# Attention loops with bodies of 12 quads in place of 4, and one rule for the score banks

## The chip, the cores and the metric

The kernel runs on one core of a Trainium2 chip. The metric is the device time of one execution in microseconds (us). The profile names the engines PE (TensorE matmuls), PEld (TensorE weight loads, which overlap PE, and with them TensorE's instruction sequencer), DVE (VectorE), ACT (ScalarE), POOL (GpSimd) and SP (SyncE).

## The reference, cut to what matters

A layer of differential attention is followed by an expert layer. Nearly all the time goes to the attention over 16 batches of 1024 tokens, with 32 score heads each (two for each of the 16 value heads):

```python
scores = jnp.einsum('bhqd,bhkd->bhqk', q, k)          # 16 x 32 heads, 1024 x 1024, hd = 8
probs = jax.nn.softmax(scores.astype(jnp.float32), axis=-1).astype(scores.dtype)
probs = probs.reshape(b, H, 2, s, s)
w = probs[:, :, 0] - lam * probs[:, :, 1]
attn = jnp.einsum('bhqk,bhkd->bhqd', w, v)
```

Behind it come an RMS norm per head, the output projection, two layer norms and the experts.

## The kernel before, in words

The stages run one after another: project (q, k and v), attend, route, experts, scatter. Only attend is touched. It works in quads of four score heads; 16 x 32 / 4 = 128 quads follow one another. Of a quad, each engine does this:

- PE, in 16 periods g = 0 to 15 of four steps x each: a score matmul of 512 columns (L894) into one of three PSUM banks `ps_e`, and a "try" matmul (L925) of the next quad into `ps_m`, whose row maxima the softmax needs. Scores and tries use different rows of the array. Twice a period four weighted sums (L911) add exponentials times v into the bank `ps_o`, two periods late (`LAG`).
- ACT takes the exponential of each score bank (L781), 64 in a quad, and copies `ps_o` out twice (L788).
- DVE takes 32 maxima (L813) of 1024 columns each, and does four short transposes (L820 twice, L825, L830).
- POOL splits the maxima into three bf16 parts and finishes the output. SP starts all DMAs: stacks of q and k four quads ahead, rows of maxima, v, totals, outputs.

The engines meet at semaphores alone. A score may be written once the exponential of the score that used the bank last is done (`exp_done`, L893); a try once the maximum of the try two before it is done (L924). Inside a loop the value waited for depends on the loop's counter, so most waits have a register instruction of their own.

Each engine has a loop of its own, with no barrier: `loops` = 128 / 4 - 1 = 31 laps with a body of `BUFS` = 4 quads, and behind it 4 quads written out. The loops are staggered. PE's body begins at g = `HEAD` = 14 of one quad and ends at g = 13 of the quad four later.
A quad has 64 scores (`HALVES`), and 4 x 64 = 256 is one more than a multiple of three (`SLOTS`). For the bank of a score to depend only on its place in the body, `bank` gives the last two scores of the body banks 0 and 2, and `scores_since` says that they and the first two of the next lap follow the last use of their bank by 2, 4, 2 and 4 scores in place of 3.

Of the kernel before, what the change touches and what calls it, by code (L numbers as in the profile page):

```python
# [25 lines left out]
ACT = mybir.ActivationFunctionType  # L26
# [8 lines left out]
TILES = S // P  # L35
# [5 lines left out]
QUAD = 4  # L41
# [28 lines left out]
STACK_DMAS = 2 * (3 + 6)  # L70
# [10 lines left out]
class Build:  # L81
# [440 lines left out]
    def attend(self, block, semaphores):  # L522
# [7 lines left out]
        nc, io, B = self.nc, self.io, self.B  # L530
        quads = B * QKH // QUAD
# [10 lines left out]
        SIDE = TRIES // 2  # L542
        BLK = 32
        BLOCKS = HALF // BLK
        loops = quads // BUFS - 1
        PE_HEAD, ACT_HEAD, DVE_HEAD = 200, 144, 192
        with ExitStack() as ctx:
            def sb(name, shape, dt=F32):
# [41 lines left out]
            passed = sem("passed")  # L590
            crossed_done, totals_moved, sums_turned = sem("crossed_done"), sem("totals_moved"), sem("sums_turned")

            def bank(u, j):

                at = HALVES * u + j
                return {BUFS * HALVES - 2: 0, BUFS * HALVES - 1: 2}.get(at, at % SLOTS)

            def scores_since(u, j):

                return {0: 2, 1: 4, BUFS * HALVES - 2: 2, BUFS * HALVES - 1: 4}.get(HALVES * u + j, SLOTS)  # L600

            @block.sync
            def _(sp):
# [39 lines left out]
                def first_half(n, u, more):  # L643
                    if more:
                        load_rows(n + AHEAD, (u + AHEAD) % BUFS, 0)
                        load_v(n + AHEAD, (u + AHEAD) % BUFS)
                    move_totals(n, 0)
# [14 lines left out]
                for u in range(FIRST_STACKS, BUFS):  # L662
                    load_stacks(u, u)
                first_half(0, 0, True)
                with hinted(nc, sp, 0, loops) as i:
                    for u in range(BUFS):
                        n = BUFS * i + u
                        second_half(n, u, True, True)
                        first_half(n + 1, (u + 1) % BUFS, True)
                        store(n, u)  # L670
                for u in range(BUFS):
                    n = BUFS * loops + u
                    if u == BUFS - 1:
                        for half in range(2):
                            sp.wait_ge(out_stored[half], 16 * QUAD * (1 + QKH // QUAD))
                        self.first_tokens(sp)
                    second_half(n, u, u < BUFS - AHEAD, False)
                    if u + 1 < BUFS:
                        first_half(n + 1, u + 1, u + 1 < BUFS - AHEAD)
                    store(n, u)  # L680
                for u in range(2):
                    sp.wait_ge(out_stored[u], 16 * QUAD * (1 + quads // 2))

# [1 line left out]
            def _(pool):  # L685
# [72 lines left out]
                pool.wait_ge(lam_done, 1)  # L758
                start, steps = 2 * AHEAD * SPLIT_STEPS, 2 * SPLIT_STEPS + FINISH_STEPS
                with hinted(nc, pool, 0, loops) as i:  # L760
                    for u in range(BUFS):
                        turn(BUFS * i + u, True, start + steps * (BUFS * i + u))
                for u in range(BUFS):
                    n = BUFS * loops + u
                    if u == BUFS - 1:
                        self.route_constants(pool)
                    turn(n, u < BUFS - AHEAD, start + steps * n - 2 * SPLIT_STEPS * max(0, u - (BUFS - AHEAD)))

            @block.scalar
            def _(act):  # L770
                act.wait_ge(lam_dots, 1)
                nc.scalar.activation(lam_exp[:], lam_dot[:], ACT.Exp).then_inc(lam_exps, 1)
                act.sem_inc(exp_done, SLOTS)
                act.sem_inc(sums_read, 1)

                def exponentials(n, u, first, end):
                    for j in range(first, end):
                        act.wait_ge(scores_done, HALVES * n + j + 1)
                        if j % QUAD == 0:
                            act.wait_ge(sums_done, GROUPS * n + j // QUAD + 1 - E_GROUPS + E_GROUPS)  # L780
                        nc.scalar.activation(e[:, j % E_BUFS], ps_e[:, bank(u, j)], ACT.Exp,  # L781
                                             scale=SCALE).then_inc(exp_done, 1)

                def copy_sums(n, c):

                    act.wait_ge(sums_done, GROUPS * n + TILES * (c + 1) + E_GROUPS)
                    act.wait_ge(crossed_done, 2 * n + 2)
                    nc.scalar.copy(sums[:, c], ps_o[:]).then_inc(sums_read, 1)  # L788

                def turn(n, u, last):  # L790
                    exponentials(n, u, COPY_AT, HALVES // 2 + COPY_AT)
                    copy_sums(n, 0)
                    exponentials(n, u, HALVES // 2 + COPY_AT, HALVES)
                    if not last:
                        exponentials(n + 1, (u + 1) % BUFS, 0, COPY_AT)
                    copy_sums(n, 1)

                exponentials(0, 0, 0, COPY_AT)
                with hinted(nc, act, 0, loops, slot=ACT_HEAD) as i:
                    for u in range(BUFS):  # L800
                        turn(BUFS * i + u, u, False)
                for u in range(BUFS):
                    turn(BUFS * loops + u, u, u == BUFS - 1)

            @block.vector
            def _(dve):
# [60 lines left out]
                        period(n + 1, u + 1, g, next_tries, rows)  # L867

                with hinted(nc, dve, 0, loops, slot=DVE_HEAD) as i:
                    for u in range(BUFS):  # L870
                        turn(BUFS * i + u, u, True, True, True)
                for u in range(BUFS - 1):
                    turn(BUFS * loops + u, u, u < BUFS - AHEAD, u + 1 < BUFS - AHEAD, u < BUFS - AHEAD)
                self.output_weights(dve)
                turn_sums(quads - 1)

# [6 lines left out]
            def _(pe):  # L883
# [2 lines left out]
                for u in range(FIRST_STACKS):  # L886
                    pe.sem_inc(stacks_loaded[u], 16 * STACK_DMAS)

                def score(n, u, j):

                    c, kt, pair, half = j // 32, j // QUAD % TILES, j // 2 % 2, j % 2
                    rows = slice(SCORE_ROW, SCORE_ROW + PRODUCTS + PARTS)
                    pe.wait_ge(exp_done, HALVES * n + j + 1 - scores_since(u, j) + SLOTS)  # L893
                    nc.tensor.matmul(ps_e[:, bank(u, j)],  # L894
                                     k_stack[rows, u, pair, c, kt * P:(kt + 1) * P],
                                     q_stack[rows, u, pair, c, half * HALF:(half + 1) * HALF],
                                     start=True, stop=True, tile_position=(SCORE_ROW, 0)).then_inc(scores_done, 1)

                def weighted_sums(i, u, g, columns):

                    n = BUFS * i + u
                    c, kt = g // TILES, g % TILES
                    if g == 0:
                        pe.wait_ge(v_loaded[u], 16 * (i + 1))
                    if kt == 0:
                        pe.wait_ge(sums_read, 2 * n + c + 1)
                    if columns.start == 0:
# [21 lines left out]
                    if half == 1:  # L929
                        last.then_inc(tries_done, 1)  # L930

                def period(i, u, g, tries, last_quad=True, this_quad=True):

                    n = BUFS * i + u
                    i2, u2 = i + (u + AHEAD) // BUFS, (u + AHEAD) % BUFS
                    if g % TILES == 0 and this_quad:
                        pe.wait_ge(rows_loaded[g // TILES][u], 16 * (i + 1))
                    if g == 0 and tries:
                        pe.wait_ge(stacks_loaded[u2], 16 * STACK_DMAS * (i2 + 1))
                    for x in range(QUAD):  # L940
                        done = (g - LAG) % GROUPS

                        columns = {(0, False): slice(0, HALF // 2), (2, False): slice(HALF // 2, HALF),
                                   (2, True): slice(0, HALF)}.get((x, done % TILES == 0))
                        if columns is not None:
                            if g >= LAG and this_quad:
                                weighted_sums(i, u, done, columns)
                            elif g < LAG and last_quad:
                                weighted_sums(i - (u == 0), (u - 1) % BUFS, done, columns)
                        if this_quad:  # L950
                            score(n, u, QUAD * g + x)
                        if tries:
                            attempt(n + AHEAD, u2, 2 * g + x // 2, x % 2)

# [5 lines left out]
                for g in range(HEAD):  # L960
                    period(0, 0, g, True, last_quad=False)

                def turn(i, u, tries, next_tries, next_quad):
                    for g in range(HEAD, GROUPS):
                        period(i, u, g, tries)
                    for g in range(HEAD if next_quad else LAG):
                        period(i + (u + 1) // BUFS, (u + 1) % BUFS, g, next_tries, this_quad=next_quad)

                with hinted(nc, pe, 0, loops, slot=PE_HEAD) as i:
                    for u in range(BUFS):  # L970
                        turn(i, u, True, True, True)
                for u in range(BUFS):
                    turn(loops, u, u < BUFS - AHEAD, u + 1 < BUFS - AHEAD, u + 1 < BUFS)

    def route(self, block, semaphores):
# [760 lines left out]
```

## Time and profile before

| what | value |
|---|---|
| median of 3 runs | 5913.19 us (5902.31 to 5917.62) |
| span of the profiled execution, first to last instruction | 5905.1 us |
| median less that span | 8.1 us |
| PE busy | 5596.0 us (95%) |
| DVE busy | 5463.9 us (93%) |
| ACT busy | 4958.8 us (84%) |
| POOL busy | 2055.8 us (35%) |
| instruction fetches of queue q8 | 457 packets, 7.49 MB |

Shares are of the span. Matmuls overlap one another, and their ends are modelled, so a busy PE is not a PE at its peak. Instructions of the sequencers (waits, register sums, branches) are not counted as busy. The page has no time for what lies around the span. The 8.1 us between it and the median is less than the 15.3 us between the lowest and the highest run.

### The profile page before, as it was taken

How to read it: one execution, taken by the hardware profiler on the slowest of the kernel's cores; microseconds unless marked ns; L12 is line 12 of the kernel's file. 1: busy time of each engine (PE TensorE's matmuls, PEld its weight loads, DVE VectorE, ACT ScalarE, POOL GpSimd, SP SyncE). 2: the span in 40 equal slices, each digit the busy share in tenths (PEclk: the TensorE clock that was granted, in tenths of full speed). 3: DMA queues.
4: the chain of work that ended last, by engine and by line, in shares of the span. 5: the costliest groups of instructions: out<-in, count | busy, mean ns of one | idle time of the engine just before them, and what ended most of it. 6: DMA issues, size and time to landing. Idle time of an engine off the chain costs nothing. (4 is left out here: it accounts for less than half of the span.)

```text
span 5905.1 us, 167685 instructions
## 1 busy us (share of the span) xinstructions
PE 5596.0 (95%) x50896; PEld 1970.1 (33%) x50896; DVE 5463.9 (93%) x6142; ACT 4958.8 (84%) x9174; POOL 2055.8 (35%) x3526
## 2 busy tenths in 40 slices
PE   8989999999999999999999999999999999997776
PEld 5542333333333333333333333333333333335425
DVE  7879999999999999999999999999999999977716
ACT  6758999999999999999999999999999999983313
POOL 7972223223332222322333222232333322226506
PEclk9989999999999999999999999999999999998878
DMA  5663222222222222232232222223222222215587
GB/s 194 222 193 58 50 50 52 53 53 53 52 53 52 49 50 51 53 53 53 53 52 53 51 50 51 51 53 53 53 53 53 51 52 51 50 47 183 199 350 301
DMA packets 408166, 495.27 MB, mean 84 GB/s; under 512 B 132051, under 2 KB 265331, under 8 KB 395235
## 3 DMA queue, kind: packets, MB, share of 16 engines
q1 hardware_dynamic: 406499, 485.74, 33.4%
q8 instruction: 457, 7.49, 0.5%
q14 instruction: 186, 1.52, 0.1%
q10 hardware_dynamic: 1024, 0.53, 0.0%
HBM read 360.60 MB, written 123.21 MB: 82 GB/s over the span
## 5 line engine op out<-in xcount | busy, mean ns | idle before, releaser
L813 DVE TENSOR_REDUCE largest<-at_ps_m 128x1 f32<-128x1024 f32 x4080 | 4676.3, 1210 | 45.1 <-PE at_ps_m L925 37.0
L781 ACT ACTIVATE at_e<-at_ps_e 128x512 f32<-128x512 f32 x8192 | 4409.0, 597 | 354.1 <-PE at_ps_e L894 145.0
L911 PE MATMUL at_ps_o<-at_e,at_v 128*32 128x256 f32 (+1 forms) x30720 | 2685.5, 421 | 32.2 <-ACT at_e L781 22.2
L894 PE MATMUL at_ps_e<-w_first 51*128 51x512 bf16 x8192 | 2515.0, 382 | 8.0 <-issue 2.4
L925 PE MATMUL at_ps_m<-w_first 48*128 48x512 bf16 x8160 | 2470.2, 383 | 54.5 <-DVE largest L813 50.5
L911 PEld LDWEIGHTS at_ps_o<-at_e,at_v 128*32 128x32 f32 x30720 | 849.0, 149 | 1566.3 <-issue 824.8
L894 PEld LDWEIGHTS at_ps_e<-w_first 51*128 51x128 bf16 x8192 | 561.2, 93 | 1668.9 <-ACT at_e L781 1637.9
L698 POOL TENSOR_TENSOR at_negated<-at_zeros,at_largest_t 128x32 f32<-128x32 f32 x256 | 64.8, 253 | 2150.6 <-DVE at_largest_t L820 2150.5
L925 PEld LDWEIGHTS at_ps_m<-w_first 48*128 48x128 bf16 x8160 | 564.8, 93 | 171.3 <-DVE largest L813 166.8
L741 POOL TENSOR_TENSOR at_rms<-at_mean_eps,at_minus_half 128x16 f32<-128x16 f32 x128 | 372.7, 2912 | 10.0
L717 POOL TENSOR_TENSOR at_crossed<-at_totals 128x32 f32<-128x32 f32 x128 | 32.4, 253 | 779.4 <-DMA at_totals<-at_sums 779.4
L451 PE MATMUL pr_ps_q<-pr_xn_t,pr_w 128*128 128x512 f32 x512 | 233.5, 599 | 12.1 <-ACT pr_xn_t L316 12.1
L715 POOL TENSOR_TENSOR at_crossed<-at_sums 128x512 f32<-128x512 f32 x128 | 164.5, 1285 | 182.8 <-ACT at_sums L788 182.8
L1160 ACT ACTIVATE ro_x<-ro_ps_y,ro_y_bias,ro_y_rstd 128x256 f32<-128x256 f32 x128 | 61.8, 565 | 150.2 <-POOL ro_y_bias L1122 150.2
L266 POOL TENSOR_TENSOR pr_rotated<-pr_rotated,pr_from_odd 128x1024 f32<-128x1024 f32 x64 | 169.3, 2647 | 34.1 <-DVE pr_from_odd L401 34.1
L735 POOL TENSOR_TENSOR at_square<-at_square 128x128 f32<-128x128 f32 (+3 forms) x512 | 157.8, 308 | 40.2
L271 POOL TENSOR_TENSOR pr_parts<-pr_rest,pr_parts 128x1024 bf16<-128x1024 f32 x64 | 166.1, 2596 | 10.6 <-ACT pr_parts L326 10.6
L322 ACT CAST pr_parts<-pr_rotated 128x1024 bf16<-128x1024 f32 x64 | 66.7, 1043 | 110.5 <-POOL pr_rotated L266 94.2
L722 POOL TENSOR_TENSOR at_second<-at_crossed_t,at_neg_lam 128x256 f32<-128x256 f32 x128 | 78.7, 614 | 219.9 <-DVE at_crossed_t L825 219.9
L788 ACT COPY at_sums<-at_ps_o 128x512 f32<-128x512 f32 x256 | 149.0, 582 | 1.2 <-PE at_ps_o L911 1.2
L1278 PE MATMUL ro_ps_y<-ro_wo,ro_attn 128*128 128x256 f32 x512 | 118.9, 389 | 16.8 <-ACT ro_x L1160 15.8
L451 PEld LDWEIGHTS pr_ps_q<-pr_xn_t,pr_w 128*128 128x128 f32 x512 | 96.6, 191 | 113.9 <-issue 93.0
(131 smaller groups left out, 3042.0 us busy)
## 6 DMA issues: line engine op xcount, KB each, us to landing
w_first<-k_parts SPq DMA_DIRECT2D x1536, 64.0 KB
w_first<-q_parts SPq DMA_DIRECT2D x256, 192.0 KB
w_first<-q_parts SPq DMA_DIRECT2D x256, 128.0 KB
w_first<-in_w SPq DMA_DIRECT2D x32, 1024.0 KB, 23.5
ex_w_second<-in_w SPq DMA_DIRECT2D x32, 1024.0 KB, 25.8
q_parts<-pr_parts SPq DMA_DIRECT2D x96, 256.0 KB, 2.5
k_parts<-pr_parts SPq DMA_DIRECT2D x96, 256.0 KB, 2.5
pr_x_in<-in_x SPq DMA_DIRECT2D x16, 1024.0 KB, 5.7
```

The costliest lines, as they stand in the source:

```text
L266: nc.gpsimd.tensor_tensor(out, out, from_odd[:, ch % 2], ALU.add if ch % 2 else ALU.subtract).then_inc(add_done, 1)
L271: nc.gpsimd.tensor_tensor(parts[:, ch, 2], rest[:, ch % 2], parts[:, ch, 1], ALU.subtract).then_inc(part3_done, 1)
L451: last = nc.tensor.matmul(ps_q[:, ch % 2, half * HALF:(half + 1) * HALF], w[:, k, ch // KC, cols], xn_t[:, u, k, half * HALF:(half + 1) * ...
L715: nc.gpsimd.tensor_tensor(crossed[:, 0:HALF], sums[:, 0], sums[:, 1], ALU.mult).then_inc(crossed_done, 1)
L735: nc.gpsimd.tensor_tensor(square[:, :, 0:width], square[:, :, 0:width], square[:, :, width:2 * width], ALU.add).then_inc(pool_step, 1)
L741: nc.gpsimd.tensor_tensor(rms[:], mean_eps[:], minus_half[:], ALU.pow).then_inc(pool_step, 1)
L781: nc.scalar.activation(e[:, j % E_BUFS], ps_e[:, bank(u, j)], ACT.Exp, scale=SCALE).then_inc(exp_done, 1)
L788: nc.scalar.copy(sums[:, c], ps_o[:]).then_inc(sums_read, 1)
L813: nc.vector.reduce_max(largest[:, u % 2, j // SIDE, j % SIDE:j % SIDE + 1], ps_m[:, j % 2], AX.X).then_inc(max_done, 1)
L894: nc.tensor.matmul(ps_e[:, bank(u, j)], k_stack[rows, u, pair, c, kt * P:(kt + 1) * P], q_stack[rows, u, pair, c, half * HALF:(half + 1) * ...
L911: last = nc.tensor.matmul(ps_o[32 * tile:32 * tile + 32, columns], v[:, u, tile // 2, first:first + 2 * VD * TILES - kt:TILES], e[:, (QUAD ...
L925: last = nc.tensor.matmul(ps_m[:, j % 2, half * HALF:(half + 1) * HALF], q_stack[rows, u, pair, c, t * P:(t + 1) * P], k_stack[rows, u, pa ...
```

## The change

In attend the body of every engine's loop becomes `LAP` = 3 x `BUFS` = 12 quads. `loops` becomes 128 // 12 = 10, so the loops cover 120 quads, and 8 quads are written out behind them. 12 x 64 = 768 scores are a multiple of three: `scores_since` goes, every score waits for the exponential three before it, and `bank` is the count modulo three throughout. `uses` gives how often a stack's buffer has been filled, which now depends on the place in the body. `hinted` and the three head slots stay as they are. The work of a quad stays the same on every engine. The core of the diff:

```diff
-        loops = quads // BUFS - 1
+        LAP = 3 * BUFS
+        loops = quads // LAP
         PE_HEAD, ACT_HEAD, DVE_HEAD = 200, 144, 192
...
-            def bank(u, j):
-
-                at = HALVES * u + j
-                return {BUFS * HALVES - 2: 0, BUFS * HALVES - 1: 2}.get(at, at % SLOTS)
-
-            def scores_since(u, j):
-
-                return {0: 2, 1: 4, BUFS * HALVES - 2: 2, BUFS * HALVES - 1: 4}.get(HALVES * u + j, SLOTS)
+            def uses(i, k):
+
+                return LAP // BUFS * i + k // BUFS + 1
+
+            def bank(k, j):
+
+                return (HALVES * k + j) % SLOTS
...
-                    pe.wait_ge(exp_done, HALVES * n + j + 1 - scores_since(u, j) + SLOTS)
-                    nc.tensor.matmul(ps_e[:, bank(u, j)],
+                    pe.wait_ge(exp_done, HALVES * n + j + 1)
+                    nc.tensor.matmul(ps_e[:, bank(k, j)],
...
                 with hinted(nc, pe, 0, loops, slot=PE_HEAD) as i:
-                    for u in range(BUFS):
-                        turn(i, u, True, True, True)
-                for u in range(BUFS):
-                    turn(loops, u, u < BUFS - AHEAD, u + 1 < BUFS - AHEAD, u + 1 < BUFS)
+                    for k in range(LAP):
+                        turn(i, k, True, True, True)
+                for n in range(LAP * loops, quads):
+                    turn(loops, n - LAP * loops, n < quads - AHEAD, n + 1 < quads - AHEAD, n + 1 < quads)
```

The loops of SP, POOL, ACT and DVE are changed in the same way.

## Rows read from the trace of the kernel before

**Rows 1.** Busy time by stretch: before the attention's steady part, and that part.

```profile
core 0: us, PE busy (x) PEld busy (x) DVE busy (x) ACT busy (x) POOL busy (x), PEclk, DMA share, GB/s
0.00:452.00 452.00, 399.79 (x1344) 227.59 (x1344) 349.63 (x516) 282.10 (x385) 364.73 (x177) 0.94 0.62 199
452.57:5153.45 4700.88, 4618.40 (x45609) 1427.69 (x45610) 4660.85 (x4462) 4358.48 (x8184) 1371.39 (x2961) 1.00 0.27 52
```

**Rows 2.** Waits of PE from 1000 to 4500 us, then the maxima's group there.

```profile
PE at_ps_m L925 <- DVE largest L813: 35.3, 138, 0.3
PE at_ps_o L911 <- ACT at_e L781: 15.6, 21, 1.4
PE at_ps_o L911 <- issue: 6.2, 25, 0.4
...
L813 DVE TENSOR_REDUCE largest<-at_ps_m 128x1 f32<-128x1024 f32 x2958 | 3389.7, 1209 | 25.5 <-PE at_ps_m L925 19.5
```

**Rows 3.** Timeline of PE, start and us: the wide sums of g = 10, quads 40 to 44.

```profile
1995.16 1.09 PE L911 MATMUL at_ps_o<-at_e,at_v 128*32 128x512 f32 x8
2033.71 1.10 PE L911 MATMUL at_ps_o<-at_e,at_v 128*32 128x512 f32 x8
2071.38 1.10 PE L911 MATMUL at_ps_o<-at_e,at_v 128*32 128x512 f32 x8
2109.00 1.10 PE L911 MATMUL at_ps_o<-at_e,at_v 128*32 128x512 f32 x8
2146.62 1.10 PE L911 MATMUL at_ps_o<-at_e,at_v 128*32 128x512 f32 x8
```

**Rows 4.** The same for quads 124 to 126, behind the loop's last lap.

```profile
5177.43 1.10 PE L911 MATMUL at_ps_o<-at_e,at_v 128*32 128x512 f32 x8
5219.05 1.10 PE L911 MATMUL at_ps_o<-at_e,at_v 128*32 128x512 f32 x8
5256.67 1.10 PE L911 MATMUL at_ps_o<-at_e,at_v 128*32 128x512 f32 x8
```

**Rows 5.** Timeline of PE behind the branch of 2003.2 us.

```profile
2003.89 0.67 PE L911 MATMUL at_ps_o<-at_e,at_v 128*32 128x256 f32 x8 [0.27 <-issue]
2006.88 0.67 PE L911 MATMUL at_ps_o<-at_e,at_v 128*32 128x256 f32 x8 [0.64 <-ACT at_e L781]
```

**Rows 6.** Closing branches of PE's and DVE's loops: ns min/median/max, first and last start.

```profile
L969 PEldq COMPARE_BRANCH  x32: 87/357/454, 488.5 to 5185.5; - x32
...
L869 DVEq COMPARE_BRANCH  x32: 55/61/72, 484.6 to 5181.5; - x32
```

**Rows 7.** One lap of PE by stretch, then its register instructions of L893 and L924.

```profile
2003.20:2154.66 151.46, 148.85 (x1474) 46.09 (x1472) 150.43 (x145) 140.63 (x265) 44.53 (x96) 1.00 0.27 53
...
L893 PEldq ALU_OP  x7812: 32/32/36, 489.1 to 5185.3; - x196
L893 PEldq FUSED_REGOPS  x124: 37/37/51, 494.0 to 5152.7; - x124
...
L924 PEldq ALU_OP  x3813: 32/32/32, 489.9 to 5184.6; - x191
L924 PEldq FUSED_REGOPS  x155: 46/51/51, 489.2 to 5153.3; - x155
```

**Rows 8.** Fetches (packets, MB, share): 2003.2-2154.6, 1994.9-1996.0, 2004.5-2005.7, 2041.5-2042.7 us.

```profile
q8 instruction: 14, 0.23, 0.7%
...
q8 instruction: 1, 0.02, 5.4%
...
q8 instruction: 1, 0.02, 5.5%
...
q8 instruction: 1, 0.02, 6.2%
```

**Rows 9.** The loop's end: fetch 5186.8-5188.0 us, PE's timeline, busy time by stretch.

```profile
q8 instruction: 1, 0.02, 5.7%
...
5189.21 0.39 PE L894 MATMUL at_ps_e<-w_first 51*128 51x512 bf16 x1 [2.40 <-issue]
...
5191.00:5194.00 3.00, 3.00 (x22) 0.48 (x16) 2.26 (x2) 1.73 (x4) 0.00 (x0) 0.50 0.00 0
```

More of the change, by code:

```diff
@@ L664, in _, with turn @@
                 first_half(0, 0, True)
-                with hinted(nc, sp, 0, loops) as i:
-                    for u in range(BUFS):
[L667 to L670, printed above, removed]
-                for u in range(BUFS):
-                    n = BUFS * loops + u
-                    if u == BUFS - 1:
+                def turn(n, k, left):
+                    u = k % BUFS
+                    second_half(n, u, left > AHEAD, left > BUFS)
+                    if left > 1:
+                        first_half(n + 1, (u + 1) % BUFS, left > 1 + AHEAD)
+                    store(n, u)
+                with hinted(nc, sp, 0, loops) as i:
+                    for k in range(LAP):
+                        turn(LAP * i + k, k, quads)
+                for k in range(quads - LAP * loops):
+                    n, left = LAP * loops + k, quads - LAP * loops - k
+                    if left == 1:
                         for half in range(2):
@@ L676, in _ @@
                         self.first_tokens(sp)
[L677 to L680, printed above, removed]
+                    turn(n, k, left)
                 for u in range(2):
@@ L760, in _ @@
                 with hinted(nc, pool, 0, loops) as i:
[L761 to L765, printed above, removed]
+                    for k in range(LAP):
+                        turn(LAP * i + k, True, start + steps * (LAP * i + k))
+                for n in range(LAP * loops, quads):
+                    if n == quads - 1:
                         self.route_constants(pool)
-                    turn(n, u < BUFS - AHEAD, start + steps * n - 2 * SPLIT_STEPS * max(0, u - (BUFS - AHEAD)))
+                    turn(n, n < quads - AHEAD, start + steps * n)
             @block.scalar
@@ L774, in _, with exponentials @@
                 act.sem_inc(sums_read, 1)
-                def exponentials(n, u, first, end):
+                def exponentials(n, k, first, end):
                     for j in range(first, end):
@@ L780, in exponentials @@
                             act.wait_ge(sums_done, GROUPS * n + j // QUAD + 1 - E_GROUPS + E_GROUPS)
-                        nc.scalar.activation(e[:, j % E_BUFS], ps_e[:, bank(u, j)], ACT.Exp,
+                        nc.scalar.activation(e[:, j % E_BUFS], ps_e[:, bank(k, j)], ACT.Exp,
                                              scale=SCALE).then_inc(exp_done, 1)
@@ L788, in copy_sums, with turn @@
                     nc.scalar.copy(sums[:, c], ps_o[:]).then_inc(sums_read, 1)
-                def turn(n, u, last):
-                    exponentials(n, u, COPY_AT, HALVES // 2 + COPY_AT)
+                def turn(n, k, last):
+                    exponentials(n, k, COPY_AT, HALVES // 2 + COPY_AT)
                     copy_sums(n, 0)
-                    exponentials(n, u, HALVES // 2 + COPY_AT, HALVES)
+                    exponentials(n, k, HALVES // 2 + COPY_AT, HALVES)
                     if not last:
-                        exponentials(n + 1, (u + 1) % BUFS, 0, COPY_AT)
+                        exponentials(n + 1, k + 1, 0, COPY_AT)
                     copy_sums(n, 1)
@@ L799, in _ @@
                 with hinted(nc, act, 0, loops, slot=ACT_HEAD) as i:
[L800 to L803, printed above, removed]
+                    for k in range(LAP):
+                        turn(LAP * i + k, k, False)
+                for n in range(LAP * loops, quads):
+                    turn(n, n - LAP * loops, n == quads - 1)
             @block.vector
@@ L869, in _ @@
                 with hinted(nc, dve, 0, loops, slot=DVE_HEAD) as i:
[L870 to L873, printed above, removed]
+                    for k in range(LAP):
+                        turn(LAP * i + k, k, True, True, True)
+                for n in range(LAP * loops, quads - 1):
+                    turn(n, n % BUFS, n < quads - AHEAD, n + 1 < quads - AHEAD, n < quads - AHEAD)
                 self.output_weights(dve)
@@ L887, in _, with score @@
                     pe.sem_inc(stacks_loaded[u], 16 * STACK_DMAS)
-                def score(n, u, j):
+                def score(n, k, j):
+                    u = k % BUFS
                     c, kt, pair, half = j // 32, j // QUAD % TILES, j // 2 % 2, j % 2
                     rows = slice(SCORE_ROW, SCORE_ROW + PRODUCTS + PARTS)
-                    pe.wait_ge(exp_done, HALVES * n + j + 1 - scores_since(u, j) + SLOTS)
-                    nc.tensor.matmul(ps_e[:, bank(u, j)],
+                    pe.wait_ge(exp_done, HALVES * n + j + 1)
+                    nc.tensor.matmul(ps_e[:, bank(k, j)],
                                      k_stack[rows, u, pair, c, kt * P:(kt + 1) * P],
@@ L897, in score, with weighted_sums @@
                                      start=True, stop=True, tile_position=(SCORE_ROW, 0)).then_inc(scores_done, 1)
-                def weighted_sums(i, u, g, columns):
-                    n = BUFS * i + u
+                def weighted_sums(i, k, g, columns):
+                    n, u = LAP * i + k, k % BUFS
                     c, kt = g // TILES, g % TILES
                     if g == 0:
-                        pe.wait_ge(v_loaded[u], 16 * (i + 1))
+                        pe.wait_ge(v_loaded[u], 16 * uses(i, k))
                     if kt == 0:
@@ L930, in attempt, with period @@
                         last.then_inc(tries_done, 1)
-                def period(i, u, g, tries, last_quad=True, this_quad=True):
-                    n = BUFS * i + u
-                    i2, u2 = i + (u + AHEAD) // BUFS, (u + AHEAD) % BUFS
+                def period(i, k, g, tries, last_quad=True, this_quad=True):
+                    n, u, u2 = LAP * i + k, k % BUFS, (k + AHEAD) % BUFS
                     if g % TILES == 0 and this_quad:
-                        pe.wait_ge(rows_loaded[g // TILES][u], 16 * (i + 1))
+                        pe.wait_ge(rows_loaded[g // TILES][u], 16 * uses(i, k))
                     if g == 0 and tries:
-                        pe.wait_ge(stacks_loaded[u2], 16 * STACK_DMAS * (i2 + 1))
+                        pe.wait_ge(stacks_loaded[u2], 16 * STACK_DMAS * uses(i, k + AHEAD))
                     for x in range(QUAD):
@@ L946, in period @@
                             if g >= LAG and this_quad:
-                                weighted_sums(i, u, done, columns)
+                                weighted_sums(i, k, done, columns)
                             elif g < LAG and last_quad:
-                                weighted_sums(i - (u == 0), (u - 1) % BUFS, done, columns)
+                                weighted_sums(i, k - 1, done, columns)
                         if this_quad:
-                            score(n, u, QUAD * g + x)
+                            score(n, k, QUAD * g + x)
                         if tries:
@@ L961, in _, with turn @@
                     period(0, 0, g, True, last_quad=False)
-                def turn(i, u, tries, next_tries, next_quad):
+                def turn(i, k, tries, next_tries, next_quad):
                     for g in range(HEAD, GROUPS):
-                        period(i, u, g, tries)
+                        period(i, k, g, tries)
                     for g in range(HEAD if next_quad else LAG):
-                        period(i + (u + 1) // BUFS, (u + 1) % BUFS, g, next_tries, this_quad=next_quad)
+                        period(i, k + 1, g, next_tries, this_quad=next_quad)
                 with hinted(nc, pe, 0, loops, slot=PE_HEAD) as i:
-                    for u in range(BUFS):
-                        turn(i, u, True, True, True)
-                for u in range(BUFS):
-                    turn(loops, u, u < BUFS - AHEAD, u + 1 < BUFS - AHEAD, u + 1 < BUFS)
+                    for k in range(LAP):
+                        turn(i, k, True, True, True)
+                for n in range(LAP * loops, quads):
+                    turn(loops, n - LAP * loops, n < quads - AHEAD, n + 1 < quads - AHEAD, n + 1 < quads)
     def route(self, block, semaphores):
```

## The prediction, made before the changed kernel was run

> **What bounds the kernel now.** I read the busy times by stretch first. The attention's steady part takes 4701 of 5905 us; PE is busy there for 98%, DVE for 99%, at a granted clock of 1.00 [rows 1]. The change touches nothing outside attend. Next the waits: in 3500 us PE is idle for 35.3 us behind DVE's maxima, 15.6 us behind ACT and 6.2 us for "issue", and DVE is idle for 25.5 us before its maxima [rows 2]. So two engines run almost without a gap, in step, and no body length changes their work. What a longer loop can change is what happens once a lap. That can be read on PE's timeline, because each quad has one wide sum (512 columns) at g = 10, ahead of the place where the loop closes (g = 14). From quad to quad these marks are 38.55, 37.67, 37.62 and 37.62 us apart [rows 3]. The first of the four intervals has the loop's branch in it. From quad 40 to quad 124 there are 21 laps: (5177.43 - 1995.16) / 21 = 151.54 us a lap [rows 3, 4]. Four quads at the 37.62 us of an interval with nothing of the loop in it are 150.48 us, so a lap loses 151.54 - 150.48 = 1.06 us. The written-out quads behind the loop take 37.62 us too (5256.67 - 5219.05) [rows 4], so that is the floor that any body length leaves.
>
> **Part 1: fewer taken branches.** 31 laps have 30 taken closing branches; 10 laps have 9. 21 x 1.06 = 22.2 us less. Where the 1.06 us sits: PE's branch takes 0.357 us (median), and PE is then idle for 0.27 us; three microseconds on it is idle for another 0.64 us [rows 5, 6]. The view puts that second gap down to an exponential, but I take it for an instruction fetch: a fetch is under way from 2004.5 to 2005.7, and none of the earlier exponentials is late. The head lies at slot 200, so only 56 instructions stand ahead of the next block's boundary; the next block is fetched only once the branch is taken, and arrives late. PE goes on 1.2 us after that fetch has ended (2006.88 - 2005.7). Since head and slot stay, each remaining edge keeps its 1.06 us.
>
> **Part 2: the score banks.** The interval that holds the two tight waits at the end of the body (quad 43 to 44) is 37.62 us long, just as its neighbour without them [rows 3]. So I cost the rule at 0. The cover is the stall at the first wide sum of the next quad, where PE waits anyway. Bound: the rows are read to 0.01 us, and a gap of 0.1 us that shows nowhere in the sum could give 31 x 0.1 = 3 us at most, and lose none.
>
> **Part 3: the end of the loop.** The interval with the branch that is not taken is 5219.05 - 5177.43 = 41.62 us, 4.00 us over the floor [rows 4]. PE stops for 2.40 us ahead of 5189.21, a fetch is under way from 5186.8 to 5188.0, and from 5191 to 5194 the granted clock is 0.50, the lower level of 1.2 GHz, where it was 1.00 before that idle time [rows 9]. The cause is where the branch lies. A lap has 1472 matmuls, 1472 weight loads, (7812 + 124 + 3813 + 155) / 31 = 384 register instructions for scores and tries [rows 7], and 36 others (waits and register sums of L906, L908, L937, L939, and the loop's own four): 3364. That fits 14 fetches of one block each [rows 8]. From slot 200 on, the branch is at 200 + 3363 = 13 x 256 + 235: slot 235 of the last block. That block's one fetch (at 1994.9, the block having been entered 236 instructions ahead of 2003.2, at about 1992.6) brings the head; the block behind the loop isn't there when the loop ends 20 instructions short of it. In the changed kernel the body is 3 x 3360 + 4, some 10,080 instructions, and the branch is at 200 + 10,080 = 40 x 256 + 40: slot 40. After the last lap over 200 instructions remain, at 151.5 / 3364 = 45 ns each some 9.6 us; the fetch needs about 1.3 (branch to fetch, 5185.5 to 5186.8) + 1.1 + 1.2 us. So the 4.00 us go. Bounds 2.4 (the idle time alone) to 4.0; I take 4.0.
>
> **Part 4: the head is fetched late.** The same slot works the other way on the 9 taken branches. PE reaches the branch 40 instructions into the last block, 1.4 to 1.8 us after entering it; before it had 236 instructions, over 10 us. The head's fetch begins only after that entry: 1994.9 less 1992.6 = 2.3 us after it before. Another block, entered 824 instructions behind the head of 2003.6 (37 us, so near 2041), has its successor's fetch at 2041.5, within 0.5 to 1 us [rows 8]; its place in the quad's pattern is near to that of the new last block (801 of 840 instructions past g = 14). Counted from entry, the head is then usable at 0.9 + 1.1 + 1.2 = 3.2 us (2.8 to 4.6), and PE waits 3.2 - 1.6 = 1.6 us more at each edge (1.0 to 3.2). DVE and ACT wait with it and give nothing back, since the floor is theirs too. 9 x 1.65 = 15 us (9 to 29; 0 if the head comes earlier than I read).
>
> The Trainium skill (Runtime: NRT & Kernel Launch, "Instruction fetch mechanics") says that prefetch is purely sequential and a taken branch out of the two pages at hand has to fetch its target before it goes on. This trace disagrees for the hinted loop: its edge costs 1.06 us, less than one fetch with its two latencies (3.6 us at the loop's end). Its 256 instructions to a block agree with the 14 fetches. By its rule, 21 edges fewer would have been worth 21 x 3.6 = 76 us.
>
> **Part 5: the other engines.** ACT's and POOL's bodies grow three times, with the branch many microseconds behind its block's entry at some 4 and 1 instructions per us, so a fetch of 2 to 3 us is hidden. DVE's 295 instructions become some 880; its branch takes 0.061 us now [rows 6], and 44 instructions at 2 per us give 20 us of cover. SP feeds rows about ten microseconds ahead of use. I cost all at 0, with 1 to 3 us at each of 9 edges (9 to 27 us) if DVE's cover fails. Of the written-out quads there are 8 in place of 4, with fewer register instructions and no change of pace.
>
> **Sum.** On the profiled span: -22.2 + 0 - 4.0 + 15 + 0 = -11 us, so 5905.1 becomes 5894. The median of the runs lies 8.1 us above the span and I carry that over: 5913.2 - 11 = 5902 us.
>
> **The rivals.**
> (a) The head is there in time: the hint brings it while PE is still in the block before. Then part 4 is 0: 5913.2 - 26.2 = 5887 us. For it: fetches of other blocks begin within half a microsecond of entry. Against it: 14 blocks, 14 fetches in a lap, and the one in the last block is the head's, 2.3 us into it.
> (b) The slower side: the stall at each edge is as long as the one at the loop's end, and the clock falls as it did there. With the head's fetch 2.3 us after entry, PE waits 3.2 us, and the lower clock adds 4.0 - 2.7 = 1.3 us: 9 x 4.5 = 40 us, 5913.2 - 26.2 + 40 = 5927 us. It decides from 26.2 / 9 = 2.9 us per edge; above (26.2 + 17.7) / 9 = 4.9 us the kernel is slower by more than 0.3%. For it: the last block's delay of 2.3 us is a lap's longest that I have a row for. Against it: at the same place in the pattern it is shorter.
> (c) DVE's or SP's fetches are seen: 5902 + 9 to 27 = 5911 to 5929 us.
> (d) The change doesn't do what it says: the 1.06 us belongs to the place in the batch and not to the branch. Then nothing moves, 5913 us. The written-out quads, and three of four in a lap, speak against it.
>
> **How the numbers follow.** Forecast 47% (5902, own range 5895 to 5913); (a) 28%; (b) 14%; (c) 6%; (d) 5%. The range takes in (a) and most of (b), with the 3 us of part 2 and the spread of a median: 5884 to 5927 us. A measurement of this kernel tells about 0.3% (17.7 us) from no change, that is 5895.5 and 5930.9. Faster by more than that: (a) and a tenth of the forecast, 0.32. Slower: about half of (b) and a third of (c), with some for what I haven't thought of: 0.10. The rest, 0.58, lies within.
>
> **What would show it.** Right: marks 37.62 us apart all through the body, ten intervals with more; 41 fetches a lap of PE, the closing branch longer than 0.357 us (near 2 us) nine times; no interval of 41.6 us behind the last lap. (a): branch still 0.36 us, edge interval 38.6 us. (b): idle gaps of 3 us and granted clock of 0.50 behind each branch. Wrong altogether: a floor other than 37.62 us in the middle of the body.

## The result, and the profile after

| | before | after |
|---|---|---|
| median of 21 runs | 5908.47 us (5902.31 to 5917.62) | 5915.33 us (5905.60 to 5929.43) |
| span of the profiled execution | 5905.1 us | 5903.5 us |
| after / before | | 1.0013, 95% interval 1.0008 to 1.0019 |

By the ratio the change costs 7.7 us (5 to 11). The forecast was 11 us less. The time lies in the stated range and within the 0.3% that I called the same, but the sign is wrong. The profiled execution of after is the fastest of its 21 runs, which spread over 24 us where those of before spread over 15; its span is 9.7 us below that of the median run (5913.2 us).

PE's marks of after at g = 10, for quads 23 to 26 and then 120 and 121 (timeline, start in us; L911 is now L912):

```profile
1349.51 1.10 PE L912 MATMUL at_ps_o<-at_e,at_v 128*32 128x512 f32 x8
1387.12 1.10 PE L912 MATMUL at_ps_o<-at_e,at_v 128*32 128x512 f32 x8
1428.35 1.09 PE L912 MATMUL at_ps_o<-at_e,at_v 128*32 128x512 f32 x8
1466.02 1.10 PE L912 MATMUL at_ps_o<-at_e,at_v 128*32 128x512 f32 x8
...
5030.89 1.10 PE L912 MATMUL at_ps_o<-at_e,at_v 128*32 128x512 f32 x8
5069.27 1.10 PE L912 MATMUL at_ps_o<-at_e,at_v 128*32 128x512 f32 x8
```

The floor of 37.62 us stands, and inside a body next to nothing is lost: the intervals without a branch have a mean of 37.63 us. The interval with the taken branch is 41.23 us long where it was 38.55 [rows 3]; the nine of them are 40.4 to 42.5 us, mean 41.55, against a mean of 38.61 for the 30 before. The interval behind the last lap fell from 41.62 to 38.38 us [rows 4]. What happens at an edge, the place where a lap ends and the next one begins (branches of PE's loop; timeline behind the branch of 1395.17; busy time by stretch before, in and behind the stop; the head's fetch, 1394.9 to 1396.2; PE's fetches in the lap 939.84 to 1395.17):

```profile
L969 PEldq COMPARE_BRANCH  x11: 88/2304/3521, 487.1 to 5038.9; - x11
...
1397.75 1.09 PE L912 MATMUL at_ps_o<-at_e,at_v 128*32 128x256 f32 x8 [2.16 <-issue]
...
1380.00:1394.00 14.00, 13.72 (x138) 4.36 (x136) 13.97 (x15) 13.10 (x25) 5.98 (x12) 1.00 0.50 74
1395.60:1397.60 2.00, 0.00 (x0) 0.00 (x0) 1.58 (x2) 0.89 (x2) 0.00 (x0) 1.00 0.28 77
1398.00:1401.00 3.00, 3.00 (x22) 0.48 (x16) 1.12 (x1) 1.08 (x2) 0.00 (x0) 0.50 0.07 18
...
q8 instruction: 1, 0.02, 5.6%
...
q8 instruction: 41, 0.67, 0.7%
```

The branch takes 2.30 us in the median, against 0.357 [rows 6]. PE stands still for 2.16 us, against 0.27 [rows 5]. Behind that the granted clock is 0.50 for three microseconds (1.2 GHz after an idle stretch, 2.4 GHz before it), and a group of eight sums of 256 columns takes 1.09 us in place of 0.67. In the attention before, the only such place was the loop's end [rows 9]. The 41 fetches are one to a block of the new body.

At seven of the nine edges the head's fetch begins 0.1 to 0.3 us ahead of the branch. At the other two it begins 1.0 us behind it, and PE stands still for 3.4 and 3.45 us. One of these, the branch of 1850.25 (PE's timeline, then the fetches of 1851.2 to 1852.4 us; from 1848 to 1851.2 us q8 has none):

```profile
1854.12 0.67 PE L912 MATMUL at_ps_o<-at_e,at_v 128*32 128x256 f32 x8 [3.45 <-issue]
...
q8 instruction: 1, 0.02, 5.1%
```

### The profile page after: what moved, and what is told of

Read it like the earlier page. It is cut to its first block and busy times, and to the rows that moved or that the text cites. A ratio compares the mean times of both kernels' runs of the same rounds, so it can differ in the third digit from the quotient of the medians.

```text
span 5903.5 us, 166180 instructions
## 1 busy us (share of the span) xinstructions
PE 5589.9 (95%) x50896; PEld 1969.8 (33%) x50896; DVE 5461.2 (93%) x6142; ACT 4961.3 (84%) x9174; POOL 2050.3 (35%) x3526
## 5 line engine op out<-in xcount | busy, mean ns | idle before, releaser
L912 PE MATMUL at_ps_o<-at_e,at_v 128*32 128x256 f32 (+1 forms) x30720 | 2690.2, 422 | 26.0 <-issue 22.6
L912 PEld LDWEIGHTS at_ps_o<-at_e,at_v 128*32 128x32 f32 x30720 | 849.0, 149 | 1562.8 <-issue 860.9
```

The lines of the kernel that those rows point to most:

```text
L912: last = nc.tensor.matmul(ps_o[32 * tile:32 * tile + 32, columns], v[:, u, tile // 2, first:first + 2 * VD * TILES - kt:TILES], e[:, (QUAD ...
```

## The experiments

**PE alone, the others alone.** PE's loop gets 12 quads in `laps` = 10 laps, the other four keep 4, and so do the special score banks:

```diff
...
-                with hinted(nc, pe, 0, loops, slot=PE_HEAD) as i:
-                    for u in range(BUFS):
+                with hinted(nc, pe, 0, laps, slot=PE_HEAD) as i:
+                    for k in range(LAP):
...
```

> PE's loop alone has a body of 12 quads, the loops of ACT, DVE, POOL and SP keep 4, and the score banks keep their special rule every four quads. Theory (it is all PE's branch): edge intervals 41.6 us as in the changed kernel, 9 of them, time as the changed kernel, ratio 1.001. Rival (DVE's, ACT's or SP's longer bodies, which are no longer held whole, cost part of it): edge intervals shorter, ratio 0.997 to 0.999.

Measured 1.0008 (0.9999 to 1.0017). Of nine edge intervals the shortest is 40.9, the longest 45.0 us, mean 42.6. So PE's loop by itself does what the change does. This profiled execution, with a span of 5916.8 us, is the slowest of this kernel's 11 runs, and its edges cost 5.0 us each where those of after's profile, the fastest of its runs, cost 3.9. Of these 1.1 us, 0.5 are longer stops of PE, because the head's fetch begins up to 1.2 us behind the branch; the lower clock comes behind all nine stops, and longer. I take it that this is what spreads the runs; two profiles of two kernels don't show it. The longest stop:

```profile
945.15 1.09 PE L918 MATMUL at_ps_o<-at_e,at_v 128*32 128x256 f32 x8 [4.20 <-issue]
...
945.20:948.20 3.00, 3.00 (x22) 0.57 (x24) 0.92 (x1) 1.09 (x2) 0.00 (x0) 0.50 0.10 25
```

The counterpart, with PE at 4 quads (its head at slot 95), the four others at 12, and the special banks again:

> The counterpart of the run in which PE alone had 12 quads: ACT, DVE, POOL and SP have bodies of 12 quads, PE has 4 with its head at slot 95 (branch at slot 130), and the banks keep the special rule every four quads. Theory (the others' longer bodies and their fetches are hidden): as the kernel with bodies of 4 and PE's head at slot 95, ratio 0.9945, all edges of PE 0.15 us over 37.62, save for the end of ACT's loop, where a fetch may come late once (up to 5 us, as seen with slot 35: 0.999 of the ratio). Rival (DVE, no longer held whole, or SP costs time at its 9 edges): 9 intervals longer by 1 us or more, ratio 0.996 to 0.999.

Measured 0.9956 (0.9943 to 0.9970), what the theory gives with its one late fetch. The interval reaches into the rival's range, so it is the profile that decides. All edges of PE but one are 37.76 to 37.80 us, and none of the others' nine edges shows. That one interval, behind the end of the others' loops, is 43.35 us: ACT stands still for 3.6 us there. It is the only cost of any size that the profile shows of the longer bodies of ACT, DVE, POOL and SP, 5.7 us once.

**The slot of the branch, at 12 quads.**

```diff
-        PE_HEAD, ACT_HEAD, DVE_HEAD = 200, 144, 192
+        PE_HEAD, ACT_HEAD, DVE_HEAD = 35, 144, 192
```

> The changed kernel with the head of PE's loop at slot 35 in place of 200; its body of 10,080 instructions then closes at slot 130. Theory (the head's block is fetched only once PE is in the last block, and the branch at slot 39 comes before it): 130 instructions, 5.8 us, stand ahead of the branch and 126 behind it, so neither the taken branches nor the end of the loop wait for a fetch, and 221 instructions stand behind the head. Branch back to about 0.36 us, edge intervals 37.9 to 38.0 us, no interval of 41 us, granted clock 1.00 throughout the loop. Sum against the kernel before: -30 x 1.06 + 9 x 0.3 - 4.0 = -33 us, ratio 0.9944. Rival (what costs is the longer body itself: more code to fetch for the other engines, edges of DVE and SP): the slot changes nothing, edge intervals stay at 41.6 us, ratio 1.000 to 1.002.

Measured 0.9949 (0.9936 to 0.9963), 0.64% below the changed kernel's 1.0013, for one number. The branch's median is 357 ns again, the edge intervals are 37.76 to 37.79 us, and the granted clock is 1.00 from 458 to 5021 us. The one miss is an interval of 43.25 us behind the last lap, in which ACT, not PE, has no instruction (branches of PE's loop; marks of PE; ACT's timeline):

```profile
L969 PEldq COMPARE_BRANCH  x11: 88/357/372, 482.6 to 5000.6; - x11
...
4992.60 1.10 PE L912 MATMUL at_ps_o<-at_e,at_v 128*32 128x512 f32 x8
5035.85 1.09 PE L912 MATMUL at_ps_o<-at_e,at_v 128*32 128x512 f32 x8
...
5022.55 2.06 ACT L781 ACTIVATE at_e<-at_ps_e 128x512 f32<-128x512 f32 x4 [4.21 <-issue]
```

**The slot, at 4 quads.** The kernel before with `PE_HEAD` at 95, 4, 45 and 215; its branch then lies at slot 130, 39, 80 and 250.

> The kernel before (bodies of 4 quads) with the head of PE's loop at slot 95 in place of 200; the branch moves from slot 235 to slot 130. Theory: 161 instructions behind the head, over 7 us, cover the fetch of the block after it, so the idle time of 0.64 us three microseconds behind each branch goes; the 126 instructions behind the branch cover the fetch at the loop's end. Each of 30 edges falls from 1.06 to about 0.3 us and the end from 4.0 to 0: -23 - 4 = -27 us, ratio 0.9954. Rival (the second idle time is a wait for the exponentials, as the view has it): edges stay at 1.06 us, only the end may change, ratio 0.999 to 1.000.

Measured 0.9945 (0.9931 to 0.9958). Marks of quads 24 to 26, the first interval with the branch in it, and the branches:

```profile
1378.98 1.10 PE L911 MATMUL at_ps_o<-at_e,at_v 128*32 128x512 f32 x8
1416.75 1.10 PE L911 MATMUL at_ps_o<-at_e,at_v 128*32 128x512 f32 x8
1454.42 1.10 PE L911 MATMUL at_ps_o<-at_e,at_v 128*32 128x512 f32 x8
...
L969 PEldq COMPARE_BRANCH  x32: 88/357/372, 483.0 to 5154.9; - x32
```

An edge costs 37.77 - 37.62 = 0.15 us, with 0.05 in the interval after it, and the loop's end nothing. The short body with the right slot is as fast as the long one with the right slot.

> The kernel before (bodies of 4 quads) with the head of PE's loop at slot 4, so that the branch lies at slot 39 of its block, as in the changed kernel. Theory: each of the 30 taken branches now costs what one of the changed kernel's costs, 4.03 us in place of 1.06, with the branch at 2.1 to 3.5 us and the clock at its lower level for some microseconds behind most of them; the loop's end gets 4.0 us cheaper: +89 - 4 = +85 us, ratio 1.0144. Rival (the slot does nothing; the changed kernel's dear edges come from its long body): ratio 1.000.

Measured 1.0174 (1.0156 to 1.0192), so 92 to 113 us; the two medians lie 94 us apart. Here the short body has the long one's fault: 30 edges with intervals of 38.9 to 43.9 us, the clock at its lower level behind 27 of them. It costs somewhat more than the 85 us expected, 4.3 us an edge in the profile, the fastest of its five runs.

```profile
L969 PEldq COMPARE_BRANCH  x32: 87/2484/4028, 479.7 to 5274.9; - x32
...
1410.06 0.67 PE L911 MATMUL at_ps_o<-at_e,at_v 128*32 128x256 f32 x8 [2.30 <-issue]
```

> The kernel before with the head of PE's loop at slot 45: the branch lies at slot 80 of its block, between the 39 of the changed kernel and the 130 that costs nothing. 80 instructions are some 3.3 us. Theory (the head is usable 2.3 to 4.6 us after entry of the block, mostly 3.2): most edges are free and some wait up to 1.5 us, mean 0.3 to 0.6 us over the 0.15, ratio 0.996 to 0.998, with the branch's median still at 0.36 us and its longest over 1 us. Rival (the head is asked for at the branch or at a fixed number of instructions): all edges alike, either 0.15 us (0.9945) or 4 us (1.0144).

Measured 0.9963 (0.9950 to 0.9977), in the expected interval, but otherwise spread than expected: the edges are nearly all alike, 37.87 us (0.25), with the branch at 453 ns, and one of 30 takes 1.17 us.

```profile
L969 PEldq COMPARE_BRANCH  x32: 88/453/1168, 490.3 to 5168.4; - x32
```

The fetch of the head ends 1.2 us ahead of the branch in one lap and 2.1 in another, and the branch takes 453 ns in both. So these 0.1 us over the 357 ns aren't time spent waiting for that fetch; what they are stays open. In the lap of the 1.17 us it ends only 0.24 us ahead. So the lead that the head needs lies between 39 instructions (1.4 us, 4 us lost) and 80 (nearly free).

> The kernel before with the head of PE's loop at slot 215 in place of 200: the branch lies at slot 250, and 41 instructions in place of 56 stand between the head and the next block. Theory (the second idle time of an edge is a wait for that next block, which is fetched once the branch is taken): it comes 15 instructions = 0.67 us earlier, the fetch at the same time, so each of 30 edges costs 1.73 us in place of 1.06: +20 us, ratio 1.0034. Rival (it is a wait for exponentials, as the view has it): unchanged, ratio 1.000.

Measured 1.0077 (1.0064 to 1.0091), 46 us and not 20. The typical edge is 39.64 us, so it costs 2.02 us and not 1.73, and 6 of the 30 cost 3.7 to 4.0, with the lower clock behind them; the loop's end costs 7.45. The second idle time of an edge, the one on which the theories differ, went from 0.64 [rows 5] to 1.23 us for 15 instructions fewer behind the head:

```profile
1405.37 0.67 PE L911 MATMUL at_ps_o<-at_e,at_v 128*32 128x256 f32 x8 [0.21 <-issue]
1408.40 0.65 PE L911 MATMUL at_ps_o<-at_e,at_v 128*32 128x256 f32 x2 [1.23 <-issue]
```

In the 6 dear edges it is 1.39 to 1.77 us. It is a wait for the next block, as read, and here the view says "issue" itself. With slot 95 it is gone.

**The score banks.** The long body with slot 35, and the tight pairs back every four quads:

```diff
...
-                    pe.wait_ge(exp_done, HALVES * n + j + 1)
+                    pe.wait_ge(exp_done, HALVES * n + j + 1 - scores_since(k, j) + SLOTS)
...
```

> The changed kernel with PE's head at slot 35 and the special score banks put back every four quads (31 times). Theory (the tight wait of 0.09 us is taken back at the next quad's first wide sum): all intervals 37.62 us, time as without them, ratio 0.9949. Rival (each costs its 0.09 us and more): up to +3 us, ratio 0.9955.

Measured 0.9956 (0.9942 to 0.9970) against 0.9949 (0.9936 to 0.9963) without them: the two can't be told apart, but these intervals are 16 us wide and don't decide between 0 and the rival's 3 us. In the two profiles the time from the first mark at g = 10 to the last is 4787.6 and 4786.4 us, and the intervals with a tight pair but no branch are mostly 37.62 us, as their neighbours; the few that are longer come with and without the pairs.

**ACT's late code.** ACT's head moved as well:

```diff
-        PE_HEAD, ACT_HEAD, DVE_HEAD = 35, 144, 192
+        PE_HEAD, ACT_HEAD, DVE_HEAD = 35, 224, 192
```

> The changed kernel with PE's head at slot 35, and ACT's head at slot 224 in place of 144. With slot 35 one interval stays long, 43.25 us behind the last lap: ACT stands still for 4.21 us some 45 us after its loop has ended at slot 154, with 102 instructions to the next block. The kernels with 4 quads end ACT's loop at slot 234 and show none of this. Theory (ACT's own code comes late behind its loop, and it depends on the slot): with slot 224 ACT's loop ends at slot 234, the stop goes or falls below 1 us, the interval falls from 43.25 to under 39 us, and the ratio from 0.9949 to 0.9942. Rival (it is the 8 quads written out, or chance): the long interval stays, ratio 0.995.

Measured 0.9935 (0.9922 to 0.9949), the lowest of all, though its interval overlaps those of the two kernels at 0.9945 and 0.9949. The long interval behind the last lap is gone (37.62 us). The profile has a new one at the loop's start, 7.4 us over the floor: PE stands still for 4.5 us, which the view puts down to a transfer of maxima, and ACT and DVE wait for PE. Nothing ties it to ACT's slot, and no other profile has it. Without that first interval the time up to the last mark is 4.1 us less than in the slot 35 kernel.

That the boundary of ACT's code block decides where it stops is seen in four profiles. In each kernel whose ACT has 12 quads and slot 144, ACT's longest stop behind its loop comes exactly 102 instructions after its last branch, where the next block begins: 1.54, 4.21, 3.96 and 3.59 us (the changed kernel, slot 35, slot 35 with the banks, the others alone). With slot 224 it comes 23 instructions behind the branch and is 0.9 us. In the slot 35 kernel ACT's last instruction ahead of the stop ends at 5018.3 us, and a fetch on q14 begins only at 5020.2. In each of the four profiles one begins there 1.5 to 2.4 us before ACT goes on; that it is ACT's is my reading. Why it begins no earlier, with 45 us of time, I haven't shown.

## Why the prediction went wrong, step by step

**Floor, length and place: right.** 37.62 us inside the body, 10,080 instructions, the branch at slot 39 or 40, 41 fetches a lap.

**Part 1, fewer branches: right.** 21 edges of 1.06 us are gone: the quads in the middle of the new body, where a lap of four had its edge, lie 37.6 to 37.8 us apart. The fetch behind the second gap, which the view had put down to ACT, is shown by the runs with slots 95 and 215.

**Part 2, banks at 0: right**, as far as two profiles 1.2 us apart can tell.

**Part 3, the loop's end: right.** I took all 4.00 us, and 41.62 - 38.38 = 3.24 went. The other 0.76 isn't PE's: with PE alone at 12 quads the interval is 37.70 us. It is ACT's late code, which the changed kernel has too, in a milder form; the view puts the stop down to a score:

```profile
5058.16 10.58 ACT L781 ACTIVATE at_e<-at_ps_e 128x512 f32<-128x512 f32 x19 [1.54 <-PE at_ps_e L895]
```

**Part 4, the head's fetch: the mechanism right, the term too small. This is the step that failed.** I had 1.65 us more at each of 9 edges. In the profile it is 41.55 - 38.61 = 2.9 us more. PE's longer stop is 2.2 of these, and what follows it, the clock above all, 0.7:

- The cover. I took 1.6 us from the block's entry to the branch, between an average of 45 ns an instruction (1.8) and 1.4. The instructions at that place are denser, and 1.4 was the right end.
- The fetch. I took the head as usable 0.9 + 1.1 + 1.2 = 3.2 us after entry. At the edge of 1395.17 the block was entered near 1393.8, the fetch began at 1394.9, and PE went on at 1397.7: 3.9 us.
- The difference. The cover and the fetch together make 3.9 - 1.4 = 2.5 us from the branch to PE's next matmul. I had booked 3.2 - 1.6 = 1.6 us as coming wholly on top. But PE takes 0.7 us from the branch to its next matmul in any case (2003.2 to 2003.89 [rows 5]), and the 1.06 has these in it. So two errors cancelled by luck, and this edge's stop is 1.9 us longer, near to the 1.65.
- The late fetches. At two of the nine edges the head's fetch began 1.0 us behind the branch, and the branch took 3.5 us. That lifts the mean from 1.9 to 2.2 us. I had a range for it, 1.0 to 3.2, and took a typical edge as the mean. Why these two are late isn't shown.
- The clock. I put the drop of the clock into rival (b) alone, for stops like the 2.40 us of the loop's end, and priced the forecast's 1.65 us without it. It came behind 7 of 9 stops. Edges with the same branch of 2.25 to 2.31 us have intervals of 41.2 us (two with the lower clock) and 40.4 and 40.9 us (two without): 0.3 to 0.8 us for the clock. Behind the lower clock the second stop, the one for the next block, is under 0.2 us, so this price is what is left once that has been saved.

For a run at the median the profile gives only an estimate: its span is 9.7 us longer than the profiled one, which is 1.1 us for each of nine edges if all of it sits there, so 5.0 us an edge. The slowest run of the kernel with PE alone has 5.0 as well.

Summed up by the profile: -22.2 - 3.2 + 9 x 2.9 = +0.7 us, and the two spans differ by -1.6. By that estimate for the median: -22.2 - 3.2 + 9 x (5.0 - 1.1) = +9.7 us, against 7.7 measured.

**Part 5, the other engines: right to within one late fetch.** Their fetches rose (q14 from 148 to 373 packets between 600 and 5100 us) and cost nothing in the loop. I had not foreseen ACT's stop behind it: 0.8 us in the changed kernel, and 4.7 to 5.7 us in the three others in which ACT has 12 quads and slot 144.

**The rivals.** What happened is (b), a stop at each edge with the lower clock behind it, 2.9 us an edge on top of the 1.06 in the profile and an estimated 3.9 at the median, where I gave 4.5 on top. I gave it 14%. The argument against it, that the last block's delay is shorter at this place in the pattern, was right at seven of nine edges (1.1 us and not 2.3 at the edge above) and didn't help, since the late fetches and the clock used the margin up. Its break-even of 2.9 us per edge stood in the text, and the forecast's own range for the term (1.0 to 3.2) reached over it, so 47 to 14 was too sure. (a) is out by the branch's 2.30 us. (d) is out by the 37.6 to 37.8 us between quads where a lap of four had its edge. (c) is out, for the loop itself, by the run with the other engines alone.

## What to carry to other kernels

In these kernels a loop's edge of PE is priced by where its branch and its head lie in the fetch blocks. The hinted head is fetched only from the last block on, the block behind the head only once the branch is taken, and the one behind the loop only once it isn't. So instructions should stand before the branch in its block (39 were too few, 80 nearly enough, 130 enough), behind it (20 were too few, 125 enough) and behind the head (41 and 56 were too few, 161 enough). Whoever changes a body's length has to place the head anew: one number was worth 0.6% here. Three times as many quads in the body were worth nothing that could be measured, with the head well placed in both (0.9949 and 0.9945). And where a cost is a difference of two times (a fetch and its cover), the error of each goes whole into the result, times the number of edges, and what the old cost already holds has to come off.

## What the runs showed of the hardware that I had not expected

- PE's clock fell at 7 of 9 edges of the changed kernel, where PE had stood still for 1.9 to 3.5 us, and at 6 of the 30 edges of the slot 215 kernel, whose second stop was 1.39 to 1.77 us there, with 0.2 to 0.3 us ahead of it. Behind second stops of 1.23 us it didn't fall, and behind those of 1.50 us it fell in two laps of four. Before, it never fell at the edges, with at most 1.42 us.
- The head's fetch has no fixed time. In the kernel before it begins between 10.5 and 3.7 us ahead of the branch, mostly 8.6, the last block being entered about 10.9 us ahead. In the changed kernel and in the slot 4 kernel each of the 39 taken branches ends 1.3 to 1.6 us after that fetch has ended.
- ACT, which has some 2 instructions per microsecond there, stood still for 4.2 us for want of code behind its loop, though it had 102 instructions and 45 us to the next block.
